# Transposing the next rows by a DRAM round trip and VectorE blocks instead of TensorE, in a fused linear-attention and mixture-of-experts layer

## The reference, cut to what matters

```python
xn = _layernorm(x, axis=-1)
# attention, per batch of 512 rows
q, k, v = xn @ Wq + bq, xn @ Wk + bk, xn @ Wv + bv     # 16 heads of 16
q, k = elu(q) + 1, elu(k) + 1
kv = einsum('bkhd,bkhm->bhdm', k, v)
attn = (q @ kv) / max(q . sum(k), eps) @ Wo + bo
# feed-forward
shared = swiglu(xn @ w_in.T) @ w_out.T
h = swiglu(xn @ w1.T)
routed = sum over the row's two experts e of  weight_e * (h @ w2[e].T)
out = x + attn + shared + routed
```

## Time and profile before

| | before |
|---|---|
| median of 3 runs | 958.81 us |
| profiled execution, whole | 958.68 us |
| profiled execution, span of instructions | 956.9 us |
| mean granted TensorE clock | 0.996 |
| busy VectorE | 674.7 us (71%) |
| busy ScalarE | 364.3 us (38%) |
| busy GpSimd | 475.8 us (50%) |

### The profile page before, as it was taken

One profiled execution on the slowest core, in us unless ns is written; L12 is line 12 of the kernel. 1 busy time (PEld: TensorE's weight loads), 2 busy tenths in 40 slices (PEclk: granted clock), 3 DMA queues, 4 the chain that ended last, 5 costly groups with the idle time before them and its releaser, 6 DMA issues. The chain is left out here.

```text
span 956.9 us, 21231 instructions
## 1 busy us (share of the span) xinstructions
PE 932.7 (97%) x6302; PEld 842.8 (88%) x6303; DVE 674.7 (71%) x1724; ACT 364.3 (38%) x611; POOL 475.8 (50%) x550
## 2 busy tenths in 40 slices
PE   5999999999999999999999999999999999999995
PEld 5788989898888989898989888898979999999995
DVE  5949585867767585958586776768595777777773
ACT  5344434343525354443534352535442222222220
POOL 4846353626354453635362635444462656556654
PEclk9999999999999999999999999999999999999998
DMA  9130312111111213030211111121236677777770
GB/s 276 58 122 12 110 41 80 66 55 66 55 66 55 88 33 121 8 113 33 88 62 59 66 55 66 55 88 33 99 97 191 129 144 140 144 140 141 147 134 0
DMA packets 106262, 84.59 MB, mean 88 GB/s; under 512 B 23552, under 2 KB 97152, under 8 KB 106240
## 3 DMA queue, kind: packets, MB, share of 16 engines
q1 hardware_dynamic: 66384, 49.03, 17.1%
q0 software_dynamic: 17968, 25.32, 11.9%
q10 hardware_dynamic: 21888, 9.97, 3.8%
HBM read 45.57 MB, written 40.13 MB: 90 GB/s over the span
## 5 line engine op out<-in xcount | busy, mean ns | idle before, releaser
L327 PE MATMUL bank<-wexp_hi,xnT_hi 128*128 (+1 forms) x560 | 191.1, 341 | 0.7 <-DVE xnT_lo L1026 0.5
L329 PE MATMUL bank<-wexp_hi,xnT_lo 128*128 (+1 forms) x560 | 186.1, 332 | 0.0
L328 PE MATMUL bank<-wexp_lo,xnT_hi 128*128 (+1 forms) x560 | 185.8, 332 | 0.0
L1121 POOL TENSOR_TENSOR res<-res,bvo 128x256 f32<-128x256 f32 x64 | 52.1, 843 | 202.8 <-DMA res<-x 202.8
L1098 POOL TENSOR_TENSOR h_lo<-gated,h_hi 128x256 fp32r<-128x256 f32 x128 | 95.7, 770 | 93.6 <-ACT h_hi L647 93.2
L327 PEld LDWEIGHTS bank<-wexp_hi,xnT_hi 128*128 128x128 f32 x560 | 106.2, 190 | 13.8 <-DVE gated L863 2.1
L329 PEld LDWEIGHTS bank<-wexp_hi,xnT_lo 128*128 128x128 f32 x560 | 106.3, 190 | 10.6
L328 PEld LDWEIGHTS bank<-wexp_lo,xnT_hi 128*128 128x128 f32 x560 | 106.3, 190 | 9.5
L327 PE MATMUL bank<-xnT_hi,win_hi 128*128 128x512 f32 x256 | 102.9, 402 | 1.9 <-DVE expt L867 1.9
L328 PE MATMUL bank<-xnT_lo,win_hi 128*128 128x512 f32 x256 | 99.8, 390 | 0.0
L329 PE MATMUL bank<-xnT_hi,win_lo 128*128 128x512 f32 x256 | 99.8, 390 | 0.0
(11 more groups left out here) (186 smaller groups left out, 2483.6 us busy)
## 6 DMA issues: line engine op xcount, KB each, us to landing
xt<-x SPq DMA_DIRECT2D x16, 512.0 KB, 3.6
res<-x SPq DMA_DIRECT2D x16, 512.0 KB, 3.6
out<-res SPq DMA_DIRECT2D x16, 512.0 KB, 2.9
xt<-h_d SPq DMA_DIRECT2D x76, 64.0 KB
xt<-h_d ACTq DMA_DIRECT2D x76, 64.0 KB
kb<-h_d SPq DMA_DIRECT2D x76, 64.0 KB
kb<-h_d ACTq DMA_DIRECT2D x76, 64.0 KB
wstage<-w_exp SPq DMA_DIRECT2D x16, 256.0 KB, 3.6
```

What stands on the lines that cost most here:

```text
L327: e.matmul(to, w_hi, m_hi_, start=first_, stop=False, skip_group_check=free)
L328: e.matmul(to, w_hi, m_lo_, start=False, stop=False, skip_group_check=free)
L329: return e.matmul(to, w_lo, m_hi_, start=False, stop=last_, skip_group_check=free)
L1121: ins = pool.tensor_tensor(res[:, t, :], res[:, t, :], bo, ALU.add)
```

## The change

In batch 0 to 14 the next rows are no longer transposed on TensorE. Instead:

- the normalised rows `xn` are stored to DRAM (`xn_d`, 512 KB) and loaded back by four DMAs, one for each quarter of 64 features, so that 32x32 blocks stand where two VectorE block transposes can turn them (`x_transposed`, 128x512 elements each), into `xT`, which is the buffer `phik`. The first of the two waits for the reload (`xn_ld`) and for the four scatters of the batch (`hs_st`). They stand before and after `gate(b, 3, 1)`;
- ScalarE's `t_high` and VectorE's `t_low` read `xT` and not the banks;
- features are spread over partitions in another order, so the host lays the weights out anew (`blocks`). For batch 0 TensorE still transposes, with 32 matmuls of 32 columns against the identity (`first_transposes`) in the place of 8 transposes;
- from batch 1 on, `norm(b + 1)` stands at the beginning of VectorE's batch b, `normalise(b + 1)` after the second `k_in`, and `reciprocal_root(b + 1)` at the beginning of GpSimd's batch. `base(b - 1)`, the addition of `y` to `res`, moves from the end of batch b - 1 to behind `norm(b + 1)` in batch b. In batch 0 `norm(1)` stands after `table_rows`, `normalise(1)` before `routed_gate` 2, and `reciprocal_root(1)` after the table scatters, where it was;
- the load of the next rows waits for `x_transposed`, and TensorE waits for `mlo_rdy` later.

```diff
+        xn_blocks = xt[:, :, :].rearrange("p t d -> p (t d)").rearrange("p (b c k) -> p b c k", c=DC, k=32)
+        xT = phik[:, :, :].rearrange("p t d -> p (t d)").rearrange("p (c s) -> p c s", c=DC)
...
 SP, load(b, last):
                 if not last:
-                    sp.wait_ge(t_done, DC * (b + 1))
+                    if first_row(b):
+                        sp.wait_ge(t_done, DC)
+                    else:
+                        wait_apart(sp, xT_rdy, 2 * b)
                     sp.dma_start(xt[:, :, :], x_rows(b + 1)).then_inc(x_ld, 16)
...
+                if not last:
+                    wait_apart(sp, xn_rdy, b + 2)
+                    sp.dma_start(xn_d.rearrange("(t p) d -> p t d", p=P), xn[:, :, :]).then_inc(xn_st, 16)
+                    wait_apart(sp, xn_st, 16 * (b + 1))
+                    for i in range(4):
+                        sp.dma_start(xt[32 * i:32 * i + 32, :, :].rearrange("p t d -> p (t d)").rearrange("p (b f) -> p b f", f=D // 4),
+                                     xn_d[:, i * (D // 4):(i + 1) * (D // 4)].rearrange("(b p) f -> p b f", p=32)).then_inc(xn_ld, 16)
 PE:
-            def transposes(b):
-                pe.wait_ge(xn_rdy, b + 1)
+            def first_transposes():
+                pe.wait_ge(xn_rdy, 1)
                 for c in range(DC):
                     for t in range(TB):
-                        mm = pe.transpose(bank[2 + 2 * c][:, t * P:(t + 1) * P], xn[:, t, c * P:(c + 1) * P], ident)
+                        for i in range(4):
+                            at = i * (D // 4) + c * 32
+                            mm = pe.matmul(bank[2 + 2 * c][32 * i:32 * i + 32, t * P:(t + 1) * P], xn[:, t, at:at + 32], ident, start=True, stop=True)
                     mm.then_inc(t_done, 1)
...
-                pe.wait_ge(mlo_rdy, b + 1)
                 pe.wait_ge(qn_rdy, DC * (b + 1))
-                if not last:
-                    transposes(b + 1)
 ACT:
+            def t_high(b):
+                act.wait_ge(xT_rdy, 2 * b)
+                act.wait_ge(hid_done, HC * b)
+                act.wait_ge(rh_done, TB * b)
+                for c in range(DC):
+                    act.copy(xnT_hi[:, c, :], xT[:, c, :]).then_inc(thi, 1)
 DVE:
+            def x_transposed(b, half):
+                if half == 0:
+                    dve.wait_ge(xn_ld, 64 * b)
+                    dve.wait_ge(hs_st, 16 * TB * b)
+                dve.transpose(xT[:, :, half * 256:half * 256 + 256].rearrange("p c (b k) -> p b c k", k=32),
+                              xn_blocks[:, 8 * half:8 * half + 8, :, :]).then_inc(xT_rdy, 1)
...
+                if not first_row(b):
+                    if not last:
+                        norm(b + 1)
+                    base(b - 1)
                 for t in range(TB):
                     k_in(t)
+                    if t == 1 and not first_row(b) and not last:
+                        normalise(b + 1)
...
+                if not last:
+                    x_transposed(b + 1, 0)
                 gate(b, 3, 1)
                 if not last:
+                    x_transposed(b + 1, 1)
                     t_low(b + 1)
 POOL, batch(b, last):
+                if not first_row(b) and not last:
+                    reciprocal_root(b + 1)
```

More of the change, by code:

```diff
@@ L223, in layer_program @@
         xn_rdy = sem("xn_rdy")
+        xn_st = sem("xn_st")
+        xn_ld = sem("xn_ld")
+        xT_rdy = sem("xT_rdy")
         tlo = sem("tlo")
@@ L586, in _ @@
             pe.wait_ge(kv_w_ld, 16 * 4)
-            transposes(0)
+            first_transposes()
             pe.wait_ge(w_split, 1)
@@ L631, in high_parts, with first_high @@
                     act.copy(hi, buf).then_inc(w_round, 1)
+            def first_high():
+                for c in range(DC):
+                    act.wait_ge(t_done, c + 1)
+                    act.copy(xnT_hi[:, c, :], bank[2 + 2 * c][:, :]).then_inc(thi, 1)
             def t_high(b):
+                act.wait_ge(xT_rdy, 2 * b)
+                act.wait_ge(hid_done, HC * b)
+                act.wait_ge(rh_done, TB * b)
                 for c in range(DC):
-                    act.wait_ge(t_done, DC * b + c + 1)
-                    wait(act, hid_done, HC * b)
-                    wait(act, rh_done, TB * b)
-                    act.copy(xnT_hi[:, c, :], bank[2 + 2 * c][:, :]).then_inc(thi, 1)
+                    act.copy(xnT_hi[:, c, :], xT[:, c, :]).then_inc(thi, 1)
             def silu(b, j, gate_bank):
@@ L708, in _ @@
             high_parts(stage_q)
-            t_high(0)
+            first_high()
             act.wait_ge(in_w_ld, 16 * 2)
@@ L782, in normalise, with first_low @@
                 ins.then_inc(xn_rdy, 1)
+            def first_low():
+                for c in range(DC):
+                    dve.wait_ge(thi, c + 1)
+                    dve.tensor_tensor(xnT_lo[:, c, :], bank[2 + 2 * c][:, :], xnT_hi[:, c, :].bitcast(f32), ALU.subtract).then_inc(tlo, 1)
+            def x_transposed(b, half):
[4 more added lines that the diff above has]
+                              xn_blocks[:, 8 * half:8 * half + 8, :, :]).then_inc(xT_rdy, 1)
             def t_low(b):
@@ L786, in t_low, with base @@
                     dve.wait_ge(thi, DC * b + c + 1)
-                    dve.tensor_tensor(xnT_lo[:, c, :], bank[2 + 2 * c][:, :], xnT_hi[:, c, :].bitcast(f32), ALU.subtract).then_inc(tlo, 1)
+                    dve.tensor_tensor(xnT_lo[:, c, :], xT[:, c, :], xnT_hi[:, c, :].bitcast(f32), ALU.subtract).then_inc(tlo, 1)
+            def base(b):
+                dve.wait_ge(res_rdy, b + 1)
+                for n in range(2):
+                    dve.wait_ge(y_done, DC * b + n + 1)
+                    two = res[:, 2 * n:2 * n + 2, :].rearrange("p t d -> p (t d)")
+                    dve.tensor_tensor(two, two, bank[5 + n][:, :], ALU.add).then_inc(base_rdy, 1)
             def logits_in(b):
@@ L923, in batch @@
                 table_rows(b)
+                if first_row(b):
+                    norm(1)
                 routed_gate(b, 1, 1)
@@ L938, in batch @@
                     tile_list()
-                else:
-                    norm(b + 1)
+                if first_row(b):
+                    normalise(1)
                 routed_gate(b, 2, 7)
@@ L949, in batch @@
                     dve.tensor_tensor(qn[:, c, :], phiq[:, c, :], bank[(6, 2)[c]][:, :], ALU.mult).then_inc(qn_rdy, 1)
-                if not last:
-                    normalise(b + 1)
                 gate(b, 2, 7)
@@ L968, in batch @@
                         low(t, 0)
-                dve.wait_ge(res_rdy, b + 1)
-                for n in range(2):
-                    dve.wait_ge(y_done, DC * b + n + 1)
-                    two = res[:, 2 * n:2 * n + 2, :].rearrange("p t d -> p (t d)")
-                    dve.tensor_tensor(two, two, bank[5 + n][:, :], ALU.add).then_inc(base_rdy, 1)
+                    base(b)
             def tile_list():
@@ L1033, in _ @@
             low_parts(stage_kv, 0)
-            t_low(0)
+            first_low()
             low_parts(stage_q, len(stage_kv))
@@ L1134, in batch @@
                     scatter(tab_d, rows[:, t, :], t, row_st)
-                if not last:
-                    reciprocal_root(b + 1)
+                if first_row(b):
+                    reciprocal_root(1)
                 for t in range(TB):
@@ L1239, in chunks, with blocks @@
         return np.ascontiguousarray(w.reshape(k // 128, 128, n).transpose(1, 0, 2))
+    def blocks(w):
+        return np.ascontiguousarray(w.reshape(4, 2, 32, -1).transpose(0, 2, 1, 3).reshape(128, 2, -1))
     def every(b):
@@ L1248 @@
         "x": a["L0_attn_inputs_q"],
-        "w_k": chunks(a["L0_attn_Wk"]),
-        "w_v": chunks(a["L0_attn_Wv"]),
-        "w_q": chunks(a["L0_attn_Wq"]),
+        "w_k": blocks(a["L0_attn_Wk"]),
+        "w_v": blocks(a["L0_attn_Wv"]),
+        "w_q": blocks(a["L0_attn_Wq"]),
         "w_o": chunks(a["L0_attn_Wo"]),
-        "w_in": chunks(a["L0_ffn_w_in"].T),
+        "w_in": blocks(a["L0_ffn_w_in"].T),
         "w_out": chunks(a["L0_ffn_w_out"].T),
         "w_exp": np.concatenate([w1, w2], 1),
-        "w_rt": chunks(np.concatenate([a["L0_ffn_wg"], a["L0_ffn_we"]], 0).T),
+        "w_rt": blocks(np.concatenate([a["L0_ffn_wg"], a["L0_ffn_we"]], 0).T),
         "b_q": np.ascontiguousarray(a["L0_attn_bq"].reshape(2, 128).T),
```

8 lines of the change are left out of this document (5 added, 3 removed).

## The result

The changed kernel takes 951.34 us (median of 4 runs, 950.87 to 952.07) against 958.68 for the kernel before (4 runs, 957.08 to 959.0): a ratio of 0.9929, 95% interval 0.9914 to 0.9944. The prediction was 953.5. The profiled execution of the changed kernel took 950.94 us, of which 949.0 are the span, at a mean granted clock of 0.995.

The account below looks back on a forecast made before the run. TensorE, busy 932.7 of 956.9 us, was taken to set the time. 958.7 + 7.0 (loss in batch 0) - 12.2 (transposes gone from 14 batches) = 953.5 us; the 8-in-10 range was 950 to 962.

Parts of the forecast that it names:

- The transposes: TensorE, batches 1 to 14: removing eight transposes saves 0.87 us a batch by start distances, 12.2 us in all.
- The end of a batch: Middle batches: the first block transpose, 0.705 us, fits VectorE's gap before `gate(3)`; scatters land in time; no cost.
- The slack for the last low part: End of a middle batch: the low part comes at 368.7, TensorE wants it at 369.3, so 0.6 us.
- Rival (a): Scatters land late in 14 batches, holding VectorE and `gate(3)`: 0.85 us a batch, 965.4 us; chance 0.13.
- The start of a batch: Middle batches: rows land later, at 371.0, but `norm`, `base` and `normalise` delay nothing TensorE needs; no cost.
- the zero slack at `gate(1)`: Middle batches: VectorE ends `gate(1)` at 349.65, TensorE needs it at 349.70; the change would not touch this.
- the cover: Start of a middle batch: rows may land about 1.5 us later free; each further us costs one per batch.
- Batch 0: Loses 7.0 us, 6.0 without a clock drop; batch 1 begins at 69.5 instead of 62.54.
- GpSimd's chain of splits: Batch 0: gapless up to the scatters, so a slower start brings `rstd` at 51.1 instead of 49.93.
- the low level behind the stall: Batch 0: after a stall of over 5 us TensorE's clock drops, losing 2.1 us; total loss 7.0 instead of 6.0.
- The slower first transposes: Start of batch 0: 32 narrow matmuls take 4.0 us against 1.94 for eight transposes, 2 us more.
- The predicted single wait of 5 to 6: Batch 0: TensorE stalls once, 5 to 6 us, for `routed_gate` 2 behind `normalise(1)`, which waits for `rstd`.

Follow-up runs that it names:

- double_tr: The kernel before, with each TensorE transpose of batches 1 to 15 issued twice: 970.46 us, ratio 1.0127.
- norm_moved: The kernel before, with statistics, normalisation and the addition of y moved as in the change, transposes left on TensorE: 961.66 us, ratio 1.0036.
- gate_first: The changed kernel, with the first block transpose moved behind `gate(3)`: 947.5 us, ratio 0.988.
- low_waits: The changed kernel, with VectorE's low parts of the next rows waiting for GpSimd's last low part of h: 949.79 us, ratio 0.9922.
- xT_psum: The changed kernel, with block transposes writing PSUM banks 2 and 4 and no wait there for the scatters: 948.83 us, ratio 0.9909.
- x_late: The changed kernel, with the load of the next rows waiting for VectorE's low parts instead of the block transposes: 959.28 us, ratio 1.0006.
- rstd_early: gate_first, with `reciprocal_root(1)` ahead of the table scatters in batch 0: 945.88 us, ratio 0.9872.
- pool_delay: The changed kernel, with an unused 128x256 addition on GpSimd ahead of the activation scatters in batches 1 to 14: 956.1 us, ratio 0.9977.
- best: gate_first, rstd_early and act_high together, with batch 0's 32 narrow transposes replaced by eight full ones: 944.58 us, ratio 0.9857.
- act_high: The changed kernel, with high parts of w1's second half and w_out made on ScalarE instead of GpSimd: 950.11 us, ratio 0.9918.

## Why the prediction was right

- **The transposes: 0.87 a batch, 12.2 in all.** Right. The periods of before and double_tr differ by 0.88, and the 14 batches gave 11.9. It is a sum with two small terms in it that I had at nothing: the moved order gives another 0.12 a batch (norm_moved), and the wait ahead of `gate(3)` takes 1.3 to 2.8 us back (the changed kernel against gate_first), 1.3 of it in batch 14.
- **The end of a batch.** The gap for a block transpose, its 0.7 and the landing of the scatters (1.85 after the instruction; I took 1.3 + 0.4) were right within 0.2. The slack for the last low part, 0.6, was right too: it ends 0.57 before `m_hi` in 11 of the 13 batches, and VectorE's wait of 0.26 is covered. It fails in batches 7 and 12, by 0.55 that the trace of before could not show, since there VectorE's operand was in PSUM. I costed the two low parts by their old rows and did not ask where the new operand lies. The price was small (0.5 us in all, low_waits). The Trainium skill (SBUF — State Buffer, "Who interferes with whom") says that a VectorE instruction with two SBUF inputs contends with a GpSimd instruction that reads SBUF, and that one with at most one SBUF input, outside the 2-port performance modes, does not. The changed kernel, low_waits and xT_psum agree with that: 1.84 and 1.99 together in batch 7 with two such inputs, 1.29 and 1.44 with one, or apart.
- **Rival (a), 965.4.** Its mechanism exists, but in one batch of 14, where GpSimd's own pause of 2.13 us makes the scatters late: 44.87 against 43.59, 1.3 us.
- **The start of a batch.** Right as put: the rows came with 1.1 of VectorE idle, `normalise` moved nothing that TensorE waits for, and the zero slack at `gate(1)` was left alone. x_late shows that the cover is needed: without it the period is 0.40 longer, which is nearly half of what the change gives a batch. The price for each us beyond it was not one us a batch; 3.86 of idle time against 1.10 gave that 0.40.
- **Batch 0: 7.0 expected, 4.7 found.** The mechanism was right (norm_moved, gate_first and rstd_early show it), but its sum was off in four terms, and that it came so near is in part luck, since they cancel in part.
  - *First*, I wrote that GpSimd's chain of splits is without gaps up to its scatters, so that the slower start would bring `rstd` 1.2 later. That is the step that failed. The chain has gaps: the trace of before has an idle time of 1.91 us at 29.71, ended by the load of w_out, and in the changed kernel it is gone and GpSimd waits 1.35 for VectorE's table rows instead, ahead of its first scatter. `rstd` came 1.2 earlier than before (47.64 against 48.84), `normalise(1)` started at 48.73 instead of 51.1, and the store was issued at 50.17 instead of 52.7: 2.5 us less. The gap of w_out alone does not explain it: norm_moved has one of 2.29 and `rstd` at 47.97, and instructions of one shape differ in length too (the high part of w_out takes 2.43 before, 1.43 after).
  - *Second*, from the issue of the store to the landing of the reload it took 8.7 instead of 7.8: 0.9 more.
  - *Third*, from there to K1 it took 8.4 instead of 8.0: 0.4 more.
  - *Fourth*, the low level behind the stall, which moved K1 by 1.0 in my sum, is not in the 4.7. It came ahead of `hidden(2)`: after the wait for `gate(0)` eight matmuls stand 0.43 apart instead of 0.23, which is 1.6, but TensorE then waits another 1.32 for `routed_gate` 2, which VectorE's chain and `rstd` set. The size of that term was right: in gate_first, where the wait is a single one, the low level costs 2.2 (I took 2.1).

  Together - 2.5 + 0.9 + 0.4 - 1.0 = - 2.2, from 69.5 to 67.3. The Trainium skill (TensorE: Matmul & The Clock Gate, Part 1), on which the term leaned for its direction, is borne out in that the clock did fall.
- **The slower first transposes** were nothing in the end. The 32 narrow matmuls took 3.64, 1.7 longer than the eight, but TensorE reached the high level sooner (its matmuls stand 0.12 apart from 14.3 us on, in the kernel before only from 17.1), and by 25 us the changed kernel was 0.3 ahead.
- **How TensorE's wait in batch 0 is spread is no property of the kernel.** In kernels with the same work up to there it waits 3.38 + 1.32, 1.84 + 2.35 (pool_delay), 3.38 + 2.13 (low_waits) or 0 + 4.91 (gate_first) for `gate(0)` and `routed_gate` 2. The predicted single wait of 5 to 6 is the last form. K1 lies between 66.4 and 69.3 in them, so the 4.7 itself carries an error of 1 us or more, and differences between my variants below 1 us in batch 0 tell nothing. What makes the difference from one execution to the next was not settled; the landing of w_out, for which GpSimd waits 0 to 0.9 us in them, is what I would look at.

## What to carry to other kernels

Price an instruction that is taken off the bounding engine by the start of its neighbours, not by its duration, and then look for whoever stood behind the thing you moved: here the loss was one wait for `rstd`, behind four scatters on another engine, and behind it a gate that stood behind a reload; each hid the other, and only both edits together took it away. When an operand moves from PSUM to SBUF, look at which of GpSimd's instructions lie beside its reader. And put a wait behind, not ahead of, the instruction that TensorE needs next: gate_first is one moved line and gives half as much again as the change itself.

## What was not expected of the hardware

- VectorE and GpSimd held each other up here only with certain operands: two `tensor_tensor` of 128x512 took 1.84 instead of 1.29 us, and two of GpSimd's of 128x256 1.99 instead of 1.44, when VectorE read two SBUF tiles; with one operand in PSUM neither changed. Instruction by instruction it looks like waiting and not like sharing: where the two start together, one keeps its length and the other is 0.55 to 0.6 longer. In 12 of the 14 batches it is VectorE's first low part (1.28 instead of 0.69, GpSimd's 0.74 as ever); in 7 and 12 GpSimd's second is long (1.29) and then VectorE's second (1.23). An addition of 128x4, both inputs in SBUF, took 0.70 instead of 0.16.
- GpSimd pauses once for 2.1 to 2.2 us between two indirect DMAs, late in the loop of batches, in the kernel before and in the variants alike (at 668.22 before, 660.48 after, 655.59 in best). In all 13 traces it stands ahead of the same one, the second table scatter of batch 14. No wait in the profile explains it.
- The granted clock fell in batch 0 (0.76 from 36 to 43 us) after waits of TensorE of 3.38, 2.13 (act_high) and 1.84 us (rstd_early), and stayed at 1.00 in best, which doesn't wait there. From 50 to 57 us it was 0.52 in norm_moved (a wait of 6.30) and 0.59 in gate_first (4.91). After the wait of 2.13 at 62.92, behind a dense stretch, the matmuls kept their 0.12; after one of 2.47 at the same place x_late's did not.
- The landing of a scatter is not one number: 1.85 us after the end of the instruction in batch 7 of the changed kernel, 2.9 in batch 0 (53.84 to 56.72), beside the reload.
